# Products in couples on the two halves of TensorE's rows, with more spent waits between the pieces

## What is computed

```
Kf  = einsum('bjd,ed->bje', F, K_w)        # K_w 128 x 128
S   = einsum('bid,bjd->bij', F, Kf)        # 64 x 64 for each batch
out = einsum('bij,ijd->bid', S, W)         # W 64 x 64 x 128
out = out + einsum('bid,ed->bie', F, Q_w)  # Q_w 128 x 128
```

## Time and profile before

| | |
|---|---|
| median of 3 runs | 607.16 us |
| the profiled execution | 606.42 us |
| its span, from first to last instruction | 604.6 us |
| TensorE matmuls busy | 596.4 us (99%), 7690 matmuls |
| TensorE weight loads busy | 526.3 us (87%) |
| VectorE busy | 399.2 us (66%) |
| ScalarE busy | 401.5 us (66%) |
| mean granted TensorE clock | 0.998 |

### The profile page before, as it was taken

The page is one execution under the profiler, slowest core; times in us unless marked ns, Lnnn a source line. Parts: engine busy times, 40 slices in busy tenths (PEclk is TensorE's granted clock), DMA queues, the critical chain, the costliest instruction groups (busy, mean ns, idle before and its releaser), DMA issues.

```text
span 604.6 us, 17904 instructions
## 1 busy us (share of the span) xinstructions
PE 596.4 (99%) x7690; PEld 526.3 (87%) x7690; DVE 399.2 (66%) x412; ACT 401.5 (66%) x696; POOL 0.2 (0%) x4
## 2 busy tenths in 40 slices
PE   9999999999999999999999999999999999999995
PEld 7888989889898898988989898898988989889895
DVE  6556768567685675947749475685756768567486
ACT  7888393874938659295692947939387493865920
POOL 0000000000000000000000000000000000000000
PEclk9999999999999999999999999999999999999999
DMA  8644847457575575755657566484754857557177
GB/s 338 262 141 160 330 165 282 183 185 305 191 281 172 210 266 208 279 196 210 242 192 287 203 238 249 143 319 174 277 209 173 318 179 284 173 209 273 70 281 279
DMA packets 29452, 138.12 MB, mean 228 GB/s; under 512 B 3264, under 2 KB 3776, under 8 KB 21312
## 3 DMA queue, kind: packets, MB, share of 16 engines
q1 hardware_dynamic: 20736, 75.83, 31.8%
q10 hardware_dynamic: 8640, 61.15, 28.4%
HBM read 69.86 MB, written 67.11 MB: 227 GB/s over the span
## 4 chain that ended last, share of the span: by engine, by line
PE 98%; DVE 1%; issue 1%; DVEq 0%
PE ps L509 20%; PE ps L447 20%; PE ps L449 19%; PE ps L448 19%; PE ps L541 18%; DVE o_sb L372 1%; PE ps L576 1%; DVEq L49 0%; DVE o_sb L382 0%; PE ps L467 0%; PE ps L465 0%; PE ps L469 0%; DVE f_hi L388 0%; DVEq L115 0%
## 5 line engine op out<-in xcount | busy, mean ns | idle before, releaser
L337 DVE TENSOR_TENSOR f_lo<-f_ring,f_hi 128x1024 fp32r<-128x1024 f32 x124 | 151.8, 1224 | 168.2 <-ACT f_hi L217 166.6
L231 ACT ACTIVATE q_out<-ps 128x512 f32<-128x512 f32 x256 | 156.9, 613 | 6.6 <-PE ps L449 0.2
L222 ACT ACTIVATE kf<-ps 128x512 f32<-128x512 f32 x256 | 155.8, 609 | 3.5
L372 DVE TENSOR_TENSOR o_sb<-ps,q_out 128x1024 f32<-128x1024 f32 x127 | 145.1, 1215 | 19.4 <-PE ps L541 19.3
L240 ACT ACTIVATE s_t<-ps 128x512 f32<-128x512 f32 x32 | 19.1, 598 | 175.8 <-PE ps L509 175.8
L509 PE MATMUL ps<-f_ring,kf 128*64 128x64 f32 x4096 | 123.5, 222 | 0.3 <-issue 0.3
L509 PEld LDWEIGHTS ps<-f_ring,kf 128*64 128x64 f32 x4096 | 121.1, 138 | 2.6 <-issue 0.8
L541 PEld LDWEIGHTS ps<-s_t,w_sb 64*128 64x128 f32 x2048 | 115.6, 188 | 5.6 <-issue 5.6
L541 PE MATMUL ps<-s_t,w_sb 64*128 64x128 f32 x2048 | 118.6, 274 | 0.0
L447 PE MATMUL ps<-f_hi,k_hi 128*128 128x512 f32 x255 | 101.0, 396 | 0.0
L447 PE MATMUL ps<-f_hi,q_hi 128*128 128x512 f32 x256 | 100.0, 391 | 0.0
(11 more groups left out here) (39 smaller groups left out, 160.3 us busy)
## 6 DMA issues: line engine op xcount, KB each, us to landing
out<-o_sb SPq DMA_DIRECT2D x127, 512.0 KB, 3.5
f_ring<-f_t ACTq DMA_DIRECT2D x58, 1024.0 KB, 4.8
f_ring<-f_t SPq DMA_DIRECT2D x4, 1024.0 KB, 10.6
f_ring<-f SPq DMA_DIRECT2D x8, 256.0 KB, 5.3
w_sb<-w SPq DMA_DIRECT2D x1, 2048.0 KB, 17.8
out<-o_sb SPq DMA_DIRECT2D x2, 256.0 KB, 2.6
o_sb<-first SPq DMA_DIRECT2D x1, 192.0 KB, 2.9
o_sb<-first ACTq DMA_DIRECT2D x1, 192.0 KB, 3.4
```

The costliest lines, as they stand in the source:

```text
L222: nc.scalar.activation(kf[:, c // 2, c % 2 * CK:(c % 2 + 1) * CK, :, :].rearrange("d k h i -> d (k h i)"), ps[:, 2 * c % 8, :], COPY).then ...
L231: nc.scalar.activation(q_out[:, t % 2, :, :].rearrange("d i (h b) -> d i h b", h=2)[:, :, :, at:at + CK], q_bank(t * CHUNKS + c).rearrange ...
L337: nc.vector.tensor_tensor(f_lo[:, v % SPLIT, :], f_unit(v), f_hi[:, v % SPLIT, :].bitcast(F32), ALU.subtract).then_inc(flo_done, 1)
L372: nc.vector.tensor_tensor(o_sb[:, n % OBUF, :, :, :].rearrange("d x s b -> d s x b"), ps[:, bank:bank + 2, :].rearrange("d s (x b) -> d s ...
```

## The change

From the second tile on a product's three matmuls of 128 rows become six of 64 rows, three on the lower half of TensorE's rows and three on the upper. They are issued in couples, one matmul on each half, for two products at a time (`products`): in `first_halves(n)` the Q product of piece n is on the lower half and its K product on the upper, in `second_halves(n)` they have changed places. The second halves of a piece come behind the first halves of the next piece, and wait on the new semaphore `half_done` until their own first halves are done, so that both halves never write one bank at a time. Both results of a piece are thus done together. In the last tile the last step couples the K products of pieces 14 and 15, since their Q products come later, in `rows_tile`, as before.

The first halves of a piece wait for the copies of both the K and the Q product of four pieces earlier. The engines that refill a slot of `f_hi` and `f_lo` wait for `k_done` beside `q_done`. The spent waits are 220 for each tile in place of 108 (74 for 0, 220 for 56 and 284 for 132 in tiles 1, 2 and 15), and they begin behind the fourth piece. Counted from the source, from first score to first score there are now 1280 TensorE instructions (576 weight loads, 576 matmuls, 128 waits), which is five times 256, and the first score of a tile stands one instruction earlier in its 256 than before.

```diff
--- before.py
+++ after.py
@@ -38,9 +38,10 @@
 LATE = 2
 
 
-FILL = {1: 0, 2: 56}
-FILL.update((t, 108) for t in range(3, TILES - 1))
-FILL[TILES - 1] = 132
+EARLY = 3
+FILL = {1: 74, 2: 220}
+FILL.update((t, 220) for t in range(3, TILES - 1))
+FILL[TILES - 1] = 284
 
 BOTH = [v for v in range(FIRST, TILES * UNITS) if v in (4, 5) or v >= UNITS and v % UNITS in (0, 4, 6)]
 
@@ -95,6 +96,8 @@
         qhi_done, qlo_done = sem("qhi_done"), sem("qlo_done")
         fhi_first, fhi_dve, flo_first = sem("fhi_first"), sem("fhi_dve"), sem("flo_first")
         fhi_done, flo_done = sem("fhi_done"), sem("flo_done")
+
+        half_done = sem("half_done")
         k_done, kf_copied = sem("k_done"), sem("kf_copied")
         q_done, q_copied = sem("q_done"), sem("q_copied")
         s_done, s_copied, s_copied_act = sem("s_done"), sem("s_copied"), sem("s_copied_act")
@@ -206,6 +209,7 @@
                 act.wait_ge(f_first[c], 16)
 
                 wait(act, q_done, 2 * (c // 2 - SPLIT) + 2)
+                wait(act, k_done, 2 * (c // 2 - SPLIT) + 2)
                 nc.scalar.activation(f_hi[:, c // 2 % SPLIT, piece_cols(c)], f_cols(c), COPY).then_inc(fhi_first, 1)
 
             def split_f(v):
@@ -214,16 +218,20 @@
                 act.wait_ge(f_in[v // 2 % RING], 16 * f_loads(v))
 
                 act.wait_ge(q_done, 2 * (v - SPLIT) + 2)
+                act.wait_ge(k_done, 2 * (v - SPLIT) + 2)
                 nc.scalar.activation(f_hi[:, v % SPLIT, :], f_unit(v), COPY).then_inc(fhi_done, 1)
 
             def copy_kf(t, c):
 
-                act.wait_ge(k_done, t * CHUNKS + c + 1)
+                n = t * CHUNKS + c
+
+                act.wait_ge(k_done, n + 1 if n < TILES * CHUNKS - LATE else TILES * CHUNKS)
                 nc.scalar.activation(kf[:, c // 2, c % 2 * CK:(c % 2 + 1) * CK, :, :].rearrange("d k h i -> d (k h i)"),
                                      ps[:, 2 * c % 8, :], COPY).then_inc(kf_copied, 1)
 
             def copy_q(t, c):
-                act.wait_ge(q_done, t * CHUNKS + c + 1)
+                n = t * CHUNKS + c
+                act.wait_ge(q_done, n + 1 if n < TILES * CHUNKS - LATE else TILES * CHUNKS)
                 if c == 0:
 
                     wait(act, out_done, (t - 1) * UNITS)
@@ -326,6 +334,7 @@
 
                 dve.wait_ge(f_first[c], 16)
                 wait(dve, q_done, 2 * (c // 2 - SPLIT) + 2)
+                wait(dve, k_done, 2 * (c // 2 - SPLIT) + 2)
                 if c == 4:
 
                     dve.wait_ge(k_done, 1)
@@ -348,6 +357,7 @@
                     return
                 dve.wait_ge(f_in[v // 2 % RING], 16 * f_loads(v))
                 dve.wait_ge(q_done, 2 * (v - SPLIT) + 2)
+                dve.wait_ge(k_done, 2 * (v - SPLIT) + 2)
                 nc.vector.tensor_copy(f_hi[:, v % SPLIT, :], f_unit(v)).then_inc(fhi_dve, 1)
                 dve.wait_ge(fhi_dve, 4 + sum(1 for x in BOTH if x <= v))
                 low_unit(v)
@@ -448,6 +458,43 @@
                 nc.tensor.matmul(dst, w_hi[:, :], lo, start=False, stop=False)
                 return nc.tensor.matmul(dst, w_lo[:, :], hi, start=False, stop=True)
 
+
+
+
+            def products(step):
+                if step < TILES * CHUNKS - LATE:
+                    return (q_of(step), q_done), (k_of(step), k_done)
+                return (k_of(step), k_done), (k_of(step + 1), k_done)
+
+            def k_of(c):
+                return ps[:, 2 * c % 8, :], k_hi, k_lo, c
+
+            def q_of(c):
+                return q_bank(c), q_hi, q_lo, c
+
+            def passes(dst, w_hi, w_lo, c, rows, first):
+                hi = f_hi[rows, c // 2 % SPLIT, piece_cols(c)]
+                lo = f_lo[rows, c // 2 % SPLIT, piece_cols(c)]
+                yield nc.tensor.matmul(dst, w_hi[rows, :], hi, start=first, stop=False)
+                yield nc.tensor.matmul(dst, w_hi[rows, :], lo, start=False, stop=False)
+                yield nc.tensor.matmul(dst, w_lo[rows, :], hi, start=False, stop=not first)
+
+            def first_halves(step):
+                (a, _), (b, _) = products(step)
+                for ins_a, ins_b in zip(passes(*a, lower, True), passes(*b, upper, True)):
+                    pass
+                ins_a.then_inc(half_done, 1)
+                ins_b.then_inc(half_done, 1)
+
+            def second_halves(step):
+
+                pe.wait_ge(half_done, 2 * (step - CHUNKS + 1))
+                (a, a_sem), (b, b_sem) = products(step)
+                for ins_b, ins_a in zip(passes(*b, lower, False), passes(*a, upper, False)):
+                    pass
+                ins_b.then_inc(b_sem, 1)
+                ins_a.then_inc(a_sem, 1)
+
             def k_product(c):
                 three(ps[:, 2 * c % 8, :], k_hi, k_lo, f_hi[:, c // 2 % SPLIT, piece_cols(c)],
                       f_lo[:, c // 2 % SPLIT, piece_cols(c)]).then_inc(k_done, 1)
@@ -473,6 +520,9 @@
 
                 for c in range(CHUNKS):
                     n = t * CHUNKS + c
+                    if n == TILES * CHUNKS - 1:
+
+                        break
                     if n == 0:
                         k_halves()
                         pe.wait_ge(qlo_done, 1)
@@ -484,18 +534,28 @@
                         pe.wait_ge(flo_done, n // 2 - FIRST + 1)
                     if c >= 4:
 
-                        pe.wait_ge(kf_copied, n - 3)
+                        pe.wait_ge(kf_copied, n - 2 if n == TILES * CHUNKS - LATE else n - 3)
                     elif t >= 1:
 
                         pe.wait_ge(s_copied_act if c % 2 else s_copied, (t - 1) * 2 + c // 2 + 1)
-                    k_product(n)
-                    if c >= 4:
+                    if t == 0:
+                        k_product(n)
+                        if c >= 4:
+                            pe.wait_ge(q_copied, n - 3)
+                        q_product(n)
+                        continue
+                    if c >= 4 and n < TILES * CHUNKS - LATE:
                         pe.wait_ge(q_copied, n - 3)
-                    if t < TILES - 1 or c < CHUNKS - LATE:
-                        q_product(n)
-                    if t >= 1:
-                        for x in range(FILL[t] * c // CHUNKS, FILL[t] * (c + 1) // CHUNKS):
-                            pe.wait_ge(zeros_done, 1)
+                    first_halves(n)
+
+                    if c >= 1:
+                        second_halves(n - 1)
+
+                    a, b = max(c - EARLY, 0), CHUNKS - EARLY
+                    for x in range(FILL[t] * a // b, FILL[t] * max(c + 1 - EARLY, 0) // b):
+                        pe.wait_ge(zeros_done, 1)
+                if t >= 1:
+                    second_halves(min((t + 1) * CHUNKS - 1, TILES * CHUNKS - LATE))
 
             def scores(t, e):
```

## The result

The changed kernel takes 608.64 us (median of 20 runs, 604.99 to 610.66), the kernel before in the same comparison 607.52 us (20 runs, 606.01 to 608.16). The ratio is 1.0023, with a 95% interval of 1.0013 to 1.0033. It is 0.2% slower, where 593.2 us were forecast.

The account below looks back on a forecast made before the run. TensorE's own matmul work, busy 99% of the span, was taken as the bound; 12.5 + 2.9 - 1.5 = 13.9 us off the profiled 606.42 gave 592.5, or 593.2 as median, range 589 to 597 (chance 0.63).

Parts of the forecast that it names:

- Part 1: Products in couples: each couple loses 5.1 ns instead of 13.8, gaining 12.5 us over 1434 couples.
- The end that the prediction held for the other case: Products: a couple's loss stays at 13.8 ns and nothing is gained, the low end for the couples' gain.
- Part 2: Way from products into rows: the 0.19 us lost per tile goes, as shapes match, gaining 2.9 us.
- Part 3: Waits for results: copies, banks and slots fit; late sums delay first scores by 0.10 us a tile, 1.5 us lost.
- Part 4: TensorE's waits and instruction fetches: half_done, spent waits and extra k_done waits cost nothing; fetch gaps 0, within 1 us.
- its last term: Instruction fetches: gaps may come in more or fewer tiles, priced at 0, within 1 us either way.
- The loss stays: Products: couples keep 227 ns, only the way into rows is won, 604.3 us; chance 0.12, with nothing won 0.05.
- the increments serialize at 26.3 ns: Rival in products: more increments in six couples cost 12.6 us, leaving 605.8 us; chance of costly increments 0.06.
- The two slow rivals: Products: slot hand-over late, perhaps near 620 us, chance 0.09; couples not side by side, some 890 us, chance 0.05.
- a term of 0: Instruction fetches: a gap in more or fewer tiles, counted as 0 in the sum, within 1 us.

Follow-up runs that it names:

- half stores: The changed kernel storing only half of each row block (256 instead of 512 KB a store): 602.50 us, ratio 0.9934 to the kernel before.
- the sums first: The changed kernel with VectorE's last low part of a tile moved behind the eight sums: 605.29 us, ratio 0.9971 to the kernel before.
- border at 247: The changed kernel with VectorE's sums moved ahead and 162 instead of 74 spent waits in the second tile: 615.42 us, ratio 1.0150 to the kernel before.

## Why the prediction was wrong

**Part 1 failed, and with it nearly all of its 12.5 us, out of 13.9.** The step was the choice of 5.1 ns for the loss of a couple, from the rows. Measured in the change: 13.4 ns (226.7 a couple), 0.4 less than before, which over 1434 couples is 0.6 us and not 12.5. The row was read rightly as 111.8 ns a couple, and wrongly carried over to another type and another width. The loss goes with the type: at 512 columns it is 13.3 ns for the one-pass matmul and 2.5 for each instruction of plain float32, the type of the rows, and the same at full height as in couples. And 128 columns take 111.6 in every form of the one-pass matmul, so the 5.1 ns over the columns was most likely this floor, and a row with 128 columns could say nothing of 512. The end that the prediction held for the other case, 13.8 ns and gain nothing, was the true one. The rule of the Trainium skill (TensorE: Matmul & The Clock Gate, Part 3, The mechanism) that I read as support, that weight loads overlap only across row groups, does not explain the loss here: couples in different row groups and single matmuls at full height have the same 226.7 ns.

**Part 2 was right in mechanism and size.** The way into rows went from 0.32 to 0.23 us, and the rows' first couple gave back its 0.10 (7.34 to 7.23 us where no wait for sums is in it): 15 x 0.2 = 3 us, against 2.9.

**Part 3 was right in its chain.** No bank, no slot and no copy was late; the first sum came at 1.49 us after the rows' start for 1.54 forecast. The rows' stage lasted 7.28 us, 0.05 over its free 7.23, so the wait cost about 0.7 us and not 1.5 (the 2.1 us above are those of the weight loads, which begin to wait earlier). What was missing is what hangs on it. I wrote that the whole score stage is behind this wait, and priced it by its length. Also behind it is the fetch of the next instructions. In most tiles it starts 1.8 us after sum 4 ends, before (1.4 to 1.5 after the first score, the sum at -0.39) as after (1.6 to 1.85, the sum at -0.06). This is no fixed distance: two of the changed kernel's tiles with late sums start it at 2.2 and 2.75, with half stores it is 1.1 us in most tiles, and with the sums first eight tiles have 2.8.

**Part 4 failed in its last term.** "Within 1 us either way" for the gap of the earlier trace rows became 2.4 us in the profiled execution (scores 125.1 against 122.8), in one of the shorter runs. The term was seen, and priced from three small gaps, without asking what made them rare: in the kernel before, the fetch landed 2.4 to 2.9 us after the first score in most tiles, and a gap begins at about 2.9. There was no more than 0.1 to 0.5 us in hand, and 0.3 of it was given to later sums. The rest of part 4 held: the spent waits hold nothing up (no tile of products is faster without them), `half_done` costs nothing, and neither do the increments.

**The rivals.** "The loss stays" came true in its mechanism. Its 604.3 us was too low by 4.3 us: 3 us were won at the rows, and gaps, 0.7 us of waits for sums and the longer usual run took more than that back. That the increments serialize at 26.3 ns (the Trainium skill, TensorE: Matmul & The Clock Gate, Part 3, The cost: per-tile semaphore tail) does not show in the pace: with four in six couples the pace is the same 226.7 ns as in the series without any. The two slow rivals did not come: the couples run side by side, and the hand-over inside products is in time. The slower result came from a mechanism that I had only as a term of 0.

**What stays open.** Why a one-pass matmul loses 13.3 ns and each instruction of a plain float32 one 2.5. Why the fetch starts at 1.4 us in some tiles and at 2.4 in others with the same stores at the same times (the sums-first kernel had six of the one and then eight of the other); the trace doesn't say which transfer stood ahead. Why the fetch of a border 11 instructions further on, 0.16 us of scores, starts up to 1 us later. How much of the 1.8 us between the profiled and the median run of the changed kernel is gaps is not seen: its runs spread over 5.7 us, but only the shorter one was profiled, and the small spread with half stores (0.4 us in 4 runs) says little, since the kernel without spent waits has the same with whole stores. And whether the delay from sum 4 to the fetch is caused by the release of the scores or by the store of sum 5, which moves with it, is not separated.

## What to carry to other kernels

Before taking a loss per matmul from another stage, see that the stage's own bound isn't something else: a series of the very form (height, columns, type), 24 matmuls long, costs 5 us on the chip and would have turned 12.5 us of forecast into none. A stage of another type, at a pace that no narrower matmul beats, says nothing of one with four times the columns.

In a long unrolled program the fetch of instructions is a transfer like any other, with a due time: find for each border what it waits for and what traffic it meets, and count its slack as you would for a load of data. Where the slack is 0.1 to 0.5 us, an engine with a third of its time free is not free at that moment.

## What the runs showed of the hardware

- A one-pass matmul takes its columns at 2.4 GHz and 13.3 ns at 512 and 256 columns; 111.6 ns at 128. Full height, either weights, a half alone and a couple on two halves are all the same, so a couple does the work of one full matmul in the time of one.
- Plain float32 of 512 columns: 429.2 ns for each of its two instructions, 2.5 above its 1024 cycles.
- One fetch brings 16 KB (78 fetches, 1.28 MB), one for every 256 instructions; the Trainium skill (Runtime: NRT & Kernel Launch, Instruction fetch mechanics) says the same and that the cost of crossing is mostly hidden. In the scores, where 256 instructions last 3.8 us beside full DMA engines, it was not: up to 1.2 us a tile.
- From the end of a fetch to the next matmul behind a gap it takes about 1.4 us (1.2 to 1.6 over the gaps of all these kernels): fetch over at 3.34 and gap over at 4.80 (before, third tile), 3.68 and 5.13 (after, tile 13), 7.30 and 8.54 (border at 247).
- With whole stores the 16 DMA engines are full from before the first score to about 6 us after it, in the kernel before as in the changed one.
- Moving the border by 11 instructions, from 38 to 49, cost 8 us (ratios to before 0.9971 and 1.0102); by 15 the other way, about 3.5 us (1.0027).
